# Whole transposes beside each other in two mixtures of experts, and second-half weights fetched from DRAM tile by tile

## The chip, the core and the metric

One Trainium2 chip, of which the kernel uses one core. A core has TensorE (PE, matrix products and transposes), VectorE (DVE), ScalarE (ACT), GpSimd (POOL) and SyncE (SP), each with an instruction stream of its own. They meet only at semaphores. Sixteen DMA engines move data between DRAM and the on-chip memory (SBUF). Accumulators lie in eight PSUM banks. The metric is device microseconds (us) of one launch, lower is better.

## The reference

The input x has 4 x 256 rows of 256 numbers (1,024 tokens). Four steps add to it in turn: an attention-like map, a first mixture of experts, an edge map, a second mixture. All is float32. Only the two mixtures matter here (cut):

```
# first mixture: 8 experts of width 688, the best 2 for each token
g = einsum('th,efh->etf', xf, gate_w); u = einsum('th,efh->etf', xf, up_w)
y = einsum('etf,ehf->eth', silu(g) * u, down_w)
out = einsum('te,eth->th', combine, y)

# second mixture: 15 experts of width 176, the best 2, and one shared expert for all
for i in range(15):
    y = y + (silu(xf @ w1[i].T) * (xf @ w3[i].T) @ w2[i].T) * combine[:, i:i+1]
z = silu(xf @ sw1.T) * (xf @ sw3.T) @ sw2.T
```

Each mixture normalizes its input rows first, and its result is scaled by a gate and added to x.

## The kernel before

**Tiles and halves.** A mixture sorts the (token, expert) pairs by expert and cuts them into tiles of 128 slots. Each tile has two halves of 64 slots, and each half belongs to one expert, so that a tile has a first and a second expert. The first mixture has S0 = 20 tiles, the second S1 = 23. The tables `owner` (experts of the halves), `tok` (which row a slot reads) and `dst` (where its result goes) are made on the chip.

**One tile.** POOL gathers 128 rows from DRAM into `x_in` (`gather`, L402). PE transposes them into PSUM bank 6 (`turn_x`), DVE copies that to `xT` (`copy_xT`, L1007), PE multiplies by gate and up weights (`gate_up0` or `gate_up1`), ACT takes the tanh (`tanh_half`), DVE makes the hidden row (`hidden`), PE transposes it (`turn_h`), ACT (and DVE in the first mixture) copies it to `hT`, PE multiplies by the down weights (`down`), ACT copies the result to `y_sb`, and POOL scatters it to DRAM (`scatter`, L408).

**Halves side by side.** PE computes a tile's two halves with separate weights: each product is a pair, one using 64 columns of the array for the first half (FIRST), one the other 64 for the second (SECOND). Each float32 product of such a kind appears as two records. In the first mixture a transpose is one instruction over 128 columns (`turn`, L1165; `nc.tensor.transpose`, L1323). In the second it is cut like the products: `turn_rows` (L1299) makes two products of 64 columns with the identity.

**Two copies of the address.** All weights of the 8 or 15 experts lie in SBUF (`wgu`, `wdn`). The first half reads them in place, at an offset held in a PE register. The second half reads a staged copy at a fixed place. In the second mixture DVE copies 704 numbers per partition for gate and up (`stage_gate_up1`, L1024) and ACT 512 for down (`stage_down1`, L684), two buffers each. In the first mixture `stage_gate_up0` and `stage_down0` do this with one buffer; the change leaves them.

**Order of the work.** It is written out by hand for each engine. PE in the first mixture, step s (L1384): `turn_h(s)`, `gate_up0(s+1)`, `turn_x(s+2)`, `down0(s)`. In the second, step s (L1457): `turn_h(s)`, `gate_up_slots(s+2)`, `turn_x(s+3)`, `down(s)`. A second mixture step reads registers with `value_load` (L1344) ahead of gate-up and of down. After its 23 tiles come four tiles of the shared expert; four others were done before. `turn_x(t)` waits for its gathered rows and for the copy of tile t-1's transpose, as all share bank 6. `gate_up(t)` waits for `xT_copied`, `t+1` times. POOL's order in a step is gather (six or seven tiles ahead), then scatter.

**SyncE.** SP loads the experts' weights of the first mixture, stores rows, loads the second mixture's weights while the first runs (L356), and after the second mixture waits for all scatters (L371) and loads the results (L375). During the second mixture's steps it has nothing to do. `rows<-sums` (L369) loads 256 KB per transfer, `wgu<-results` (L376) loads 512 KB per transfer.

Of the kernel before, what the change touches and what calls it, by code (L numbers as in the profile page):

```python
# [14 lines left out]
P = 128  # L15
# [3 lines left out]
NS = NT // 2  # L19
# [20 lines left out]
FC0, FC1 = 120, P  # L40
# [48 lines left out]
def build(nc, x, xt, small, vecs, router, const_f, const_h, gu0, wd0, gu1, wd1, out):  # L89
# [16 lines left out]
    with ctx:  # L106
# [63 lines left out]
        stage_gu1 = wgu[:, spare:spare + 2 * GU1].rearrange("p (r f) -> p r f", f=GU1)  # L170
        stage_dn1 = wgu[:, spare + 2 * GU1:spare + 2 * GU1 + 2 * WD1].rearrange("p (r f) -> p r f", f=WD1)
# [63 lines left out]
        class Mixture:  # L235


            def __init__(m, n, experts, tiles, chunks, wide, ahead):
# [23 lines left out]
                m.y_stored = [sem(f"y_stored{n}{r}") for r in range(RING)]  # L262
# [3 lines left out]
                m.gu_staged, m.dn_staged = sem(f"gu_staged{n}"), sem(f"dn_staged{n}")  # L266
# [53 lines left out]
        def _(sp):  # L320
# [156 lines left out]
        def _(act):  # L477
# [206 lines left out]
            def stage_down1(t):  # L684

                expert = second_owner(m1, t)
                nc.scalar.activation(stage_dn1[:, t % 2, :], wdn[:, bass.ds(expert * WD1 + WD1, WD1)],
                                     ACT.Copy).then_inc(m1.dn_staged, 1)

            act.wait_ge(m1.experts_ready, 1)  # L690
            for n, (_, gu_a, gu_z, dn_a, dn_z) in enumerate(second_weights()):
                act.wait_ge(w1_here[n], 16 * (gu_z > gu_a) + 16 * (dn_z > dn_a))
            stage_down1(0)
            stage_down1(1)
# [3 lines left out]
            def step1(s, r):  # L698
# [17 lines left out]
        def _(dve):  # L716
# [307 lines left out]
            def stage_gate_up1(t):  # L1024

                expert = second_owner(mix[1], t)
                nc.vector.tensor_copy(stage_gu1[:, t % 2, :], wgu[:, bass.ds(expert * GU1 + GU1, GU1)]
                                      ).then_inc(mix[1].gu_staged, 1)

# [18 lines left out]
            def step0(s, r):  # L1048
                copy_hT(m, s, r)
                if s < m.S - 2:  # L1050
                    expert = second_owner(m, s + 2)
                    weights_of(dve, expert, s + 2)
# [6 lines left out]
                if s < m.S - 2:  # L1059
                    copy_xT(m, s + 2, r % 2)  # L1060
# [60 lines left out]
            dve.wait_ge(m1.experts_ready, 1)  # L1121
            for n, (_, gu_a, gu_z, dn_a, dn_z) in enumerate(second_weights()):
                dve.wait_ge(w1_here[n], 16 * (gu_z > gu_a) + 16 * (dn_z > dn_a))
            stage_gate_up1(0)
            stage_gate_up1(1)
# [4 lines left out]
            stage_gate_up1(2)  # L1130
            copy_xT(m1, 2, 0)
            hidden(m1, NS + 1, 1, m1.half)
            stage_gate_up1(3)

            def step1(s, r):
# [4 lines left out]
                if s < m1.S - 4:  # L1140
                    stage_gate_up1(s + 4)
# [20 lines left out]
        def _(pe):  # L1162
# [136 lines left out]
            def turn_rows(dst, src):  # L1299

                for part in (FIRST, SECOND):
                    last = mm(dst[part, :], src[:, part], ident, start=True, stop=True)  # L1302
                return last

            def turn_x(m, t, r):
# [3 lines left out]
                for k in range(KH):  # L1309
                    if m.n == 0:  # L1310
                        last = turn(psum[6][:, k * P:(k + 1) * P], x_in[:, r, k * P:(k + 1) * P])
                    else:
                        last = turn_rows(psum[6][:, k * P:(k + 1) * P], x_in[:, r, k * P:(k + 1) * P])
                last.then_inc(m.xT_done, 1)

            def turn_h(m, s, r):
# [3 lines left out]
                for j in range(m.chunks):  # L1320
                    bank, col = (4, j * P) if j < 4 else (5, (j - 4) * P)
                    if m.n == 0:
                        last = nc.tensor.transpose(psum[bank][0:m.wide, col:col + P],  # L1323
                                                   rows[:, j * m.wide:(j + 1) * m.wide], cf[:, C_ID:C_ID + P])
                    else:
                        last = turn_rows(psum[bank][:, col:col + P], rows[:, j * P:(j + 1) * P])
# [85 lines left out]
            def gate_up_slots(t, r):  # L1412
                at = owner(m1, t) * GU1 + GU1
                pe.wait_ge(m1.xT_copied, t + 1)
                pe.wait_ge(m1.gu_staged, t + 1)
                gate_up1(r, xT[:, r, :], lambda k: wgu[:, bass.ds(at + k * 2 * F1, 2 * F1)],
                         lambda k: stage_gu1[:, t % 2, k * 2 * F1:(k + 1) * 2 * F1])
# [18 lines left out]
            def down_shared(t):  # L1436

                def weights(j):
                    return wdn[:, j * H:(j + 1) * H]
# [17 lines left out]
            def step1(s, r):  # L1457
                turn_h(m1, s + NS, r % 2)
                if s < m1.S - 2:
# [3 lines left out]
                if s < m1.S - 3:  # L1463
                    turn_x(m1, s + 3, (r + 3) % RING)
# [3 lines left out]
                if s < m1.S:  # L1468
                    at = owner(m1, s) * WD1 + WD1
                    pe.wait_ge(m1.dn_staged, s + 1)  # L1470
                    down(m1, s + NS, lambda j: wdn[:, bass.ds(at + j * H, H)],
                         lambda j: stage_dn1[:, s % 2, j * H:(j + 1) * H])
# [80 lines left out]
```

## Time and profile before

| what | value |
|---|---|
| median of 3 runs | 384.3 us (381.86 to 384.68) |
| the profiled execution's own time | 386.76 us, span 385.0 us |
| PE busy | 332.4 us (86%), 2,484 instructions |
| DVE, ACT, POOL busy | 207.5, 152.3, 121.8 us |
| chain that ended last | PE 75%, DVE 10%, DMA 6%, issue 4%, ACT 2%, POOL 2% |
| moved by DMA | 49.47 MB, mean 129 GB/s |
| mean granted TensorE clock | 0.89 of full speed |

Times in rows count from the span's start. The first mixture's steps run from about 65 to 235 us, the second's from about 296 to 377. A PE record is as long as one instruction from its first column to its modelled end, and neighbours overlap: what an instruction costs is the distance to the next start. "x8" joins eight records. "PEld" is a weight load, which may run ahead of the products. In brackets stands how long the engine sat idle before it and what ended that. "issue" is idle time for which the profile shows no releaser.

### The profile page before, as it was taken

The numbers are of one execution on the slowest core, as the hardware profiler recorded it, in microseconds if no ns is written. First come the engines' busy times: TensorE is split into PE (matmuls) and PEld (weight loads), VectorE is DVE, ScalarE is ACT, GpSimd is POOL, SyncE is SP. The second block draws the span as 40 slices with busy tenths as digits, with TensorE's granted clock in tenths as the row PEclk, the third lists the DMA queues.
The fourth block names the chain that finished last, engine by engine and source line by source line (L and its number), as shares of the span: only waits on it lengthen the run. The fifth ranks groups of instructions, "written<-read, shape, count | busy, mean of one in ns | idle before, by whom it ended". The sixth has DMA issues, their size and how long they took to land.

```text
span 385.0 us, 7592 instructions
## 1 busy us (share of the span) xinstructions
PE 332.4 (86%) x2484; PEld 200.6 (52%) x2484; DVE 207.5 (54%) x639; ACT 152.3 (40%) x322; POOL 121.8 (32%) x118
## 2 busy tenths in 40 slices
PE   8966589999999999999999996049839999999991
PEld 6635454555555555555555554037525666666560
DVE  2678874445555544445555531783863444445337
ACT  1555221333333334433333344363611444445441
POOL 0022050214232223322211113230662677765320
PEclk9995558999999999999999999555975999999996
DMA  7999739993211271122216885321011222222136
GB/s 245 338 328 287 254 106 319 280 267 77 39 30 29 41 223 30 27 40 32 28 15 219 273 296 126 110 69 41 0 49 49 70 84 84 81 80 63 55 129 227
DMA packets 21659, 49.47 MB, mean 129 GB/s; under 512 B 2600, under 2 KB 11688, under 8 KB 20600
## 3 DMA queue, kind: packets, MB, share of 16 engines
q1 hardware_dynamic: 15192, 36.83, 29.5%
q0 software_dynamic: 6048, 11.28, 13.7%
q10 hardware_dynamic: 384, 0.90, 0.7%
q8 instruction: 22, 0.36, 0.4%
q14 instruction: 13, 0.11, 0.1%
HBM read 39.03 MB, written 9.96 MB: 127 GB/s over the span
## 4 chain that ended last, share of the span: by engine, by line
PE 75%; DVE 10%; DMA 6%; issue 4%; ACT 2%; POOL 2%; DVEq 0%; POOLq 0%; ACTq 0%; SPq 0%
PE bank L1361 24%; PE bank L1335 19%; PE bank L1401 10%; PE bank L1302 6%; PE bank L1323 4%; PE bank L1167 3%; DMA sums<-y_sb,route_dst 3%; PE bank L1227 2%; PE bank L1175 2%; DVE st L737 2%; DMA wgu<-results 1%; DVE z L815 1%; DVE rows L1068 1%; DMA x_in<-rows,route_tok 1%; PE bank L1247 1%
## 5 line engine op out<-in xcount | busy, mean ns | idle before, releaser
L1361 PE MATMUL bank<-wgu,xT 128*64 x320 | 99.8, 466 | 1.4 <-DVE xT L1010 1.3
L1361 PE MATMUL bank<-rows,xT 128*64 128x344 f32 x320 | 99.8, 466 | 0.0
L1335 PE MATMUL bank<-wdn,hT 120*64 (+2 forms) x396 | 88.3, 383 | 5.2 <-ACT hT L589 4.9
L404 POOL DMA_INDIRECT x_in<-rows,route_tok x43 | 43.0, 1000 | 90.1 <-PE bank L1167 58.1
L1361 PEld LDWEIGHTS bank<-wgu,xT 128*64 128x64 f32 x320 | 43.2, 140 | 47.7 <-issue 8.6
L1335 PEld LDWEIGHTS bank<-wdn,hT 120*64 120x64 f32 (+1 forms) x396 | 47.6, 137 | 31.0 <-issue 9.9
L1335 PE MATMUL bank<-rows,hT 120*64 120x256 f32 x240 | 56.0, 383 | 0.0
L412 POOL DMA_INDIRECT sums<-y_sb,route_dst x20 | 31.6, 1580 | 76.5 <-ACT y_sb L625 58.5
L990 DVE SCALAR_TENSOR_TENSOR hh<-th,bank 128x344 f32<-128x344 f32 x40 | 20.5, 513 | 60.9 <-ACT th L578 60.9
L1361 PEld LDWEIGHTS bank<-rows,xT 128*64 128x64 f32 x320 | 43.2, 140 | 0.0
L578 ACT ACTIVATE th<-bank 128x344 f32<-128x344 f32 x40 | 18.3, 457 | 56.1 <-PE bank L1361 56.1
L1401 PE MATMUL bank<-wgu,xT 128*64 (+1 forms) x184 | 34.8, 502 | 3.5 <-issue 1.6
L1021 DVE COPY rows<-wgu 128x688 f32 x78 | 36.7, 513 | 1.2 <-issue 1.2
L1010 DVE COPY xT<-bank 128x256 f32<-128x256 f32 x43 | 18.1, 421 | 29.1 <-PE bank L1302 29.0
L416 POOL DMA_INDIRECT results<-y_sb,route_dst x23 | 28.1, 1220 | 17.3 <-ACT y_sb L706 12.4
L1335 PEld LDWEIGHTS bank<-rows,hT 120*64 120x64 f32 x240 | 31.3, 137 | 0.0
L601 ACT ACTIVATE rows<-wdn 120x1536 f32 x20 | 29.7, 1483 | 4.0 <-issue 4.0
L625 ACT ACTIVATE y_sb<-bank,route_share 128x256 f32<-128x256 f32 x20 | 9.5, 474 | 53.1 <-PE bank L1335 50.9
L1167 PE MATMUL bank<-cf,rows 128*128 128x128 f32 x40 | 10.2, 386 | 20.3 <-ACT rows L514 14.6
L589 ACT ACTIVATE hT<-bank 128x256 f32<-128x256 f32 (+1 forms) x51 | 23.1, 452 | 3.7 <-PE bank L1323 2.1
L1335 PE MATMUL bank<-wgu,hT 128*64 128x256 f32 x92 | 23.8, 381 | 0.0
L994 DVE TENSOR_TENSOR hh<-hh,bank 128x344 f32<-128x344 f32 x40 | 20.5, 512 | 1.4
(156 smaller groups left out, 475.5 us busy)
## 6 DMA issues: line engine op xcount, KB each, us to landing
wgu<-gu SPq DMA_DIRECT2D x8, 1376.0 KB, 23.1
wdn<-wd SPq DMA_DIRECT2D x8, 720.0 KB, 27.2
wgu<-gu SPq DMA_DIRECT2D x3, 1408.0 KB, 6.4
wdn<-wd SPq DMA_DIRECT2D x5, 768.0 KB, 9.7
rows<-rows SPq DMA_DIRECT2D x8, 256.0 KB, 3.7
wgu<-results SPq DMA_DIRECT2D x4, 512.0 KB, 5.3
wgu<-gu SPq DMA_DIRECT2D x1, 1056.0 KB
rows<-xt SPq DMA_DIRECT2D x4, 256.0 KB, 7.2
```

The lines of the kernel that those rows point to most:

```text
L404: nc.gpsimd.indirect_dma_start(out=x_in[:, t % RING, :], out_offset=None, in_=rows, in_offset=bass.IndirectOffsetOnAxis(ap=m.tok[:, t:t + ...
L412: nc.gpsimd.indirect_dma_start(out=sums, out_offset=bass.IndirectOffsetOnAxis(ap=m.dst[:, s:s + 1], axis=0), in_=y_sb[:, s % RING, :], in_ ...
L416: nc.gpsimd.indirect_dma_start(out=results, out_offset=bass.IndirectOffsetOnAxis(ap=m.dst[:, s:s + 1], axis=0), in_=y_sb[:, s % RING, :], ...
L589: nc.scalar.activation(hT[0:m.wide, 0:n], psum[4][0:m.wide, 0:n], ACT.Copy, scale=0.5 / UNITS if m.n == 0 else 0.5).then_inc(m.hT_copied_a, 1)
L601: nc.scalar.activation(stage_dn0[0:FC0, :], wdn[0:FC0, bass.ds(expert * WD0, WD0)], ACT.Copy).then_inc(mix[0].dn_staged, 1)
L990: nc.vector.scalar_tensor_tensor(out=hh[:, cols], in0=th[:, cols], scalar=1.0, in1=psum[2 * c][:, 0:CH0], op0=ALU.add, op1=ALU.mult).then_ ...
L1021: nc.vector.tensor_copy(kept_gu[:, k, :], wgu[:, bass.ds(expert * GU0 + (k * 4 + 2 * c) * CH0, 2 * CH0)]).then_inc(mix[0].gu_staged, 1)
L1167: return nc.tensor.transpose(dst, src, cf[:, C_ID:C_ID + P])
L1302: last = mm(dst[part, :], src[:, part], ident, start=True, stop=True)
L1335: last = mm(psum[7][part, 0:H], hT[0:m.wide, j * P:(j + 1) * P][:, part], wd(j), start=(j == 0), stop=(j == m.chunks - 1))
L1361: last = mm(psum[2 * c + g][part, 0:CH0], xT[:, r, k * P:(k + 1) * P][:, part], w, start=(k == 0), stop=(k == KH - 1))
L1401: last = mm(psum[r][part, 0:2 * F1], src[:, k * P:(k + 1) * P][:, part], w(k), start=(k == 0), stop=(k == KH - 1))
```

## The change

Four edits.

1. In the first mixture PE's `turn_x(s+2)` moves from behind `gate_up0(s+1)` to directly behind `turn_h(s)`. DVE's `copy_xT(s+2)` moves ahead of the hidden rows of its step.
2. In the second mixture `turn_rows` goes; `turn_x` and `turn_h` use whole transposes, and `turn_x(s+3)` moves directly behind `turn_h(s)`. The hidden width is cut in two chunks of 96 instead of 128, so that `wd1` has 96 partitions, and its loads shrink from 768 to 576 KB.
3. DVE's and ACT's staging copies of the second mixture go. SP loads the second expert's weights from DRAM instead: 352 KB for gate and up, 192 KB for down, per tile, into three buffers.
4. PE waits for these loads instead of for the copies. Each load has a semaphore for its buffer.

```
+                    sp.wait_ge(m.experts_ready, 1)
+                    for t in range(m.S):
+                        expert = sp.value_load(m.owner[0:1, bass.ds(2 * t + 1, 1)], min_val=0, max_val=m.E - 1)
+                        if t >= 3:
+                            sp.wait_ge(m.gu_done, NS + t - 2)
+                        sp.dma_start(stage_gu1[:, t % 3, :], gu1[bass.ds(expert + 1, 1)].rearrange("e p n -> p (e n)")
+                                     ).then_inc(m.gu_here[t % 3], 16)
+                        if t >= 3:
+                            sp.wait_ge(m.y_done, NS + t - 2)
+                        sp.dma_start(stage_dn1[0:FC1, t % 3, :], wd1[bass.ds(expert + 1, 1)].rearrange("e p n -> p (e n)")
+                                     ).then_inc(m.dn_here[t % 3], 16)
...
-                    if s < m1.S - 2:
-                        stage_down1(s + 2)
...
             def step0(s, r):
                 copy_hT(m, s, r)
                 if s < m.S - 2:
+                    copy_xT(m, s + 2, r % 2)
...
-                if s < m1.S - 4:
-                    stage_gate_up1(s + 4)
...
                 turn_h(m, s, r)
+                if s < m.S - 2:
+                    turn_x(m, s + 2, (r + 2) % RING)
                 if s < m.S - 1:
                     gate_up0(s + 1, (r + 1) % 2)
-                if s < m.S - 2:
-                    turn_x(m, s + 2, (r + 2) % RING)
                 down0(s, r)
...
-                pe.wait_ge(m1.gu_staged, t + 1)
+                pe.wait_ge(m1.gu_here[t % 3], 16 * (t // 3 + 1))
...
                 turn_h(m1, s + NS, r % 2)
+                if s < m1.S - 3:
+                    turn_x(m1, s + 3, (r + 3) % RING)
                 if s < m1.S - 2:
                     gate_up_slots(s + 2, r % 2)
...
-                    pe.wait_ge(m1.dn_staged, s + 1)
+                    pe.wait_ge(m1.dn_here[s % 3], 16 * (s // 3 + 1))
```

`gu_done` and `y_done` count finished gate-ups and downs. With the NS = 4 shared tiles ahead, both waits of round t mean tile t-3.

## Rows read from the trace of the kernel before

**Rows 1.** Windows: one stretch of the second mixture; engines' busy us, PEclk, DMA share, GB/s

```profile
320.00:365.00 45.00, 43.77 (x446) 28.29 (x444) 20.65 (x55) 22.68 (x58) 26.90 (x24) 1.00 0.24 72
```

**Rows 2.** Timeline of PE, one step of the first mixture: start us, us, instruction

```profile
134.53 0.87 PE L1323 MATMUL bank<-cf,hh 128*120 128x128 f32 x6
...
135.33 0.50 PE L1361 MATMUL bank<-wgu,xT 128*64 x1
...
139.72 0.45 PE L1361 MATMUL bank<-wgu,xT 128*64 x1
...
140.11 0.44 PE L1167 MATMUL bank<-cf,x_in 128*128 128x128 f32 x2
...
140.48 0.43 PE L1335 MATMUL bank<-wdn,hT 120*64 x1
...
140.74 0.38 PE L1335 MATMUL bank<-wdn,hT 120*64 x1
...
142.69 0.38 PE L1335 MATMUL bank<-wdn,hT 120*64 x1
...
142.90 0.38 PE L1335 MATMUL bank<-wdn,hT 120*64 x1
...
143.22 0.87 PE L1323 MATMUL bank<-cf,hh 128*120 128x128 f32 x6
```

**Rows 3.** Timeline of DVE in the same step: the last hidden half

```profile
141.26 0.51 DVE L994 TENSOR_TENSOR hh<-hh,bank 128x344 f32<-128x344 f32 x1
```

**Rows 4.** Timeline, one step of the second mixture: PE, PEld, DVE, ACT

```profile
328.45 1.40 PE L1401 MATMUL bank<-wgu,xT 128*64 x8
...
329.68 0.61 PE L1302 MATMUL bank<-cf,x_in 128*64 128x128 f32 x8
...
330.12 0.38 PE L1335 MATMUL bank<-wdn,hT 128*64 x1
...
330.98 0.61 PE L1302 MATMUL bank<-cf,kv 128*64 128x128 f32 x8
331.09 0.42 DVE L1010 COPY xT<-bank 128x256 f32<-128x256 f32 x1 [1.25 <-PE bank L1302]
331.20 0.38 ACT L706 ACTIVATE y_sb<-bank 128x256 f32<-128x256 f32 x1 [0.60 <-PE bank L1335]
...
331.67 0.79 PEld L1401 LDWEIGHTS bank<-wgu,xT 128*64 128x64 f32 x8 [0.32 <-issue]
```

**Rows 5.** Timeline of PE: the last pair of down in tile 0 and in tile 22

```profile
298.90 0.38 PE L1335 MATMUL bank<-wdn,hT 128*64 x1
...
367.82 0.38 PE L1335 MATMUL bank<-wdn,hT 128*64 x1
```

**Rows 6.** Chain that ended last: waits for the first transfer of two bursts

```profile
240.58 3.08 DMA rows<-sums
...
371.46 3.64 DMA wgu<-results
```

**Rows 7.** Timeline of SP: four transfers issued one behind the other

```profile
371.46 1.90 SPq L376 DMA_DIRECT2D wgu<-results  x4
```

**Rows 8.** Chain: ACT reads an expert's number (from 229.68) and uses it as address

```profile
229.68 0.28 ACT y_sb L625
...
230.33 0.17 ACT rows L601
```

**Rows 9.** Page, DMA queues: packets, MB, share of 16 engines over the span

```profile
q1 hardware_dynamic: 15192, 36.83, 29.5%
q0 software_dynamic: 6048, 11.28, 13.7%
```

**Rows 10.** Timeline, start of the second mixture's tiles: DVE, then PE

```profile
283.50 0.18 DVE L932 CAST route_owner<-lower 1x46 int32<-1x46 f32 x1
...
288.11 2.61 PE L1401 MATMUL bank<-wgu,xT 128*64 x8 [1.63 <-issue]
```

**Rows 11.** Windows: a stretch ahead of a fall of PEclk from 1.00 to 0.50 (at 27.3)

```profile
20.40:27.30 6.90, 5.19 (x22) 2.93 (x21) 5.13 (x21) 3.73 (x16) 1.51 (x3) 1.00 1.02 311
```

More of the change, by code:

```diff
@@ L39 @@
 NF0, NF1 = -(-F0 // P), -(-F1 // P)
-FC0, FC1 = 120, P
+FC0, FC1 = 120, 96
 CH0 = F0 // 2
@@ L169, in build @@
         spare = free + 3 * NT * H
-        stage_gu1 = wgu[:, spare:spare + 2 * GU1].rearrange("p (r f) -> p r f", f=GU1)
-        stage_dn1 = wgu[:, spare + 2 * GU1:spare + 2 * GU1 + 2 * WD1].rearrange("p (r f) -> p r f", f=WD1)
+        stage_gu1 = wgu[:, spare:spare + 3 * GU1].rearrange("p (r f) -> p r f", f=GU1)
+        stage_dn1 = wgu[:, spare + 3 * GU1:spare + 3 * GU1 + 3 * WD1].rearrange("p (r f) -> p r f", f=WD1)
         psum = [ctx.enter_context(nc.psum_tensor(f"bank{i}", [P, 512], fp32)) for i in range(8)]
@@ L261, in __init__ @@
                 m.y_done, m.y_copied = sem(f"y_done{n}"), sem(f"y_copied{n}")
-                m.y_stored = [sem(f"y_stored{n}{r}") for r in range(RING)]
                 m.y_here = [sem(f"y_here{n}{b}") for b in range(B)]
@@ L265, in __init__ @@
                 m.half = sem(f"half{n}")
-                m.gu_staged, m.dn_staged = sem(f"gu_staged{n}"), sem(f"dn_staged{n}")
+                if n == 0:
+                    m.gu_staged, m.dn_staged = sem("gu_staged"), sem("dn_staged")
+                else:
+                    m.gu_here, m.dn_here = [sem(f"gu_here{r}") for r in range(3)], [sem(f"dn_here{r}") for r in range(3)]
+                    m.y_stored = [sem(f"y_stored{r}") for r in range(RING)]
                 W, k2 = experts, 2 * NT
@@ L683, in _ @@
                     route_exps(m1)
[L684 to L694, printed above, removed]
             tanh_half(m1, NS, 0)
@@ L1022, in stage_gate_up0 @@
                                           ).then_inc(mix[0].gu_staged, 1)
[L1024 to L1028, printed above, removed]
             m = mix[0]
@@ L1059, in step0 @@
                 if s < m.S - 2:
-                    copy_xT(m, s + 2, r % 2)
                     stage_gate_up0(s + 2, expert, 1)
@@ L1119, in _ @@
             route(m1)
[L1121 to L1125, printed above, removed]
             copy_xT(m1, 0, 0)
@@ L1129, in _ @@
             hidden(m1, NS, 0, m1.half)
-            stage_gate_up1(2)
             copy_xT(m1, 2, 0)
             hidden(m1, NS + 1, 1, m1.half)
-            stage_gate_up1(3)
             def step1(s, r):
@@ L1297, in _ @@
             FIRST, SECOND = slice(0, HALF), slice(HALF, P)
[L1299 to L1303, printed above, removed]
             def turn_x(m, t, r):
@@ L1309, in turn_x @@
                 for k in range(KH):
[L1310 to L1313, printed above, removed]
+                    last = turn(psum[6][:, k * P:(k + 1) * P], x_in[:, r, k * P:(k + 1) * P])
                 last.then_inc(m.xT_done, 1)
@@ L1321, in turn_h @@
                     bank, col = (4, j * P) if j < 4 else (5, (j - 4) * P)
[L1322 to L1326, printed above, removed]
+                    last = nc.tensor.transpose(psum[bank][0:m.wide, col:col + P],
+                                               rows[:, j * m.wide:(j + 1) * m.wide], cf[:, C_ID:C_ID + P])
                 last.then_inc(m.hT_done, 1)
@@ L1414, in gate_up_slots @@
                 pe.wait_ge(m1.xT_copied, t + 1)
-                pe.wait_ge(m1.gu_staged, t + 1)
+                pe.wait_ge(m1.gu_here[t % 3], 16 * (t // 3 + 1))
                 gate_up1(r, xT[:, r, :], lambda k: wgu[:, bass.ds(at + k * 2 * F1, 2 * F1)],
-                         lambda k: stage_gu1[:, t % 2, k * 2 * F1:(k + 1) * 2 * F1])
+                         lambda k: stage_gu1[:, t % 3, k * 2 * F1:(k + 1) * 2 * F1])
             for i in range(NT):
@@ L1438, in weights @@
                 def weights(j):
-                    return wdn[:, j * H:(j + 1) * H]
+                    return wdn[0:FC1, j * H:(j + 1) * H]
                 down(m1, t, weights, weights)
@@ L1462, in step1 @@
                     gate_up_shared(r % 2, xnT[:, NS + s + 2 - m1.S, :])
-                if s < m1.S - 3:
-                    turn_x(m1, s + 3, (r + 3) % RING)
                 if s == 0:
@@ L1469, in step1 @@
                     at = owner(m1, s) * WD1 + WD1
-                    pe.wait_ge(m1.dn_staged, s + 1)
-                    down(m1, s + NS, lambda j: wdn[:, bass.ds(at + j * H, H)],
-                         lambda j: stage_dn1[:, s % 2, j * H:(j + 1) * H])
+                    pe.wait_ge(m1.dn_here[s % 3], 16 * (s // 3 + 1))
+                    down(m1, s + NS, lambda j: wdn[0:FC1, bass.ds(at + j * H, H)],
+                         lambda j: stage_dn1[0:FC1, s % 3, j * H:(j + 1) * H])
                 else:
```

## The prediction

> **What bounds the kernel now.** I read the chain of waits first, then windows over the second mixture, then the timeline of one step in each mixture. In both mixtures the chain runs along PE. In the second, PE is busy 43.8 of 45 us at the full clock while DVE and ACT stand half idle and the DMA engines are used to 0.24 [rows 1]. So the staging copies that the change removes are beside PE, not on the path: by themselves they are worth nothing. What pays is what PE gains; what can cost is a load that PE must now wait for.
>
> **First mixture: the transposes.** A step lasts 143.22 - 134.53 = 8.69 us [rows 2]. Six transposes take 135.33 - 134.53 = 0.80 until gate-up starts, two take 140.48 - 140.11 = 0.37 until down starts. So one costs (0.80 - 0.37)/4 = 0.1075, and each visit to the transposes leaves 0.80 - 0.645 = 0.155 behind it. Ahead of it there is more: gate-up's 16 pairs follow each other by (139.72 - 135.33)/15 = 0.29, `turn_x` follows the last by 0.39, so 0.10 is lost on entering. The first pair of down behind it takes 0.26 where the others take 0.21. Now `turn_x` lies beside `turn_h`: one visit of eight in place of two. Per step that saves 0.155 + 0.10 + 0.05 = 0.30 us, leaving 8.39. It holds in steps 0 to 17, which have a `turn_x`: 18 x 0.30 = **-5.4 us**.
>
> Covered: hidden rows are needed by the next `turn_h`. DVE ends the last one at 141.77 [rows 3], 1.76 after gate-up's end (139.72 + 0.29 = 140.01). Gate-up is now followed by down alone, 12 pairs x 0.215 = 2.58, so 0.8 remains. DVE's earlier `copy_xT` falls into an idle stretch ahead of the hidden rows, and POOL's gathers, six tiles ahead, are only released earlier. Bounds: 0 if DVE or a gather is late after all, -6 if entering and leaving cost somewhat more than I read.
>
> **Second mixture: what PE has to do.** Before, a step is 331.67 - 328.45 = 3.22 [rows 4]: gate-up 1.23, `turn_x` 0.44, down 0.86, `turn_h` 0.44 (four of its pairs, like `turn_x`), and 0.25 of waiting for `copy_xT`, which DVE only starts at 331.09. After: four whole transposes in one visit, 0.10 + 4 x 0.1075 + 0.155 = 0.69, then 1.23 + 0.86: 2.78. Nothing waits for `copy_xT`, as it is made a whole gate-up and down ahead. Without `turn_x` it is 2.57. If the weights were always there, the stretch from the end of tile 0's down to that of tile 22's, 68.9 us before (367.82 - 298.90) [rows 5], would be 20 x 2.78 + 2 x 2.57 = 60.7. POOL, 26.9 busy in some 14 steps, or 1.9 a step [rows 1], allows that, as gathers run seven tiles ahead.
>
> **Second mixture: the load in the loop.** SP issues in the order gate-up(t), down(t), gate-up(t+1). Down(t-1) needs the buffer of tile t-4, so it waits for `y_done` of tile t-4, and gate-up(t), though its own buffer has been free for longer, is queued behind it on SP. PE wants gate-up(t) in step t-2. Between the end of down(t-4) and that point lie one step and the transposes, 2.78 + 0.69 = 3.47. What has to happen in that time:
> - until SP sees the end of down(t-4): ACT sees it at 331.20, 0.22 after down has made way for `turn_h` at 330.98 [rows 4].
> - issue of down(t-1), 1.90/4 = 0.47 [rows 7].
> - reading the expert's number: ACT needs from 229.68 to 230.33 for that, 0.65 [rows 8]. SP has not done it before. I take the same.
> - turning it into two DRAM addresses, and the test on `gu_done`: no row shows this. Bounds 0.1 and 0.9; I take 0.4. Together SP needs 1.5 (1.2 to 2.0).
> - issue to landing of 352 KB: 256 KB took 3.08 and 512 KB 3.64 [rows 6], so 3.29 by their slope; with a gather or the down load beside it a little more. I take 3.3, bounds 3.0 and 4.2.
> - 0.13 until PE's first pair runs, an estimate.
>
> That is 0.22 + 1.5 + 3.3 + 0.13 = 5.15 against 3.47: the load is late by 1.7 us. The loop closes over two steps: those 5.15, then gate-up 1.23 and down 0.86, make 7.24 us for two steps, 3.62 for one, against 3.22 before. Three buffers don't help, since SP's one queue ties the load of gate-up to the end of a down. Tile 4 is the first so bound and tile 22 the last, wanted in step 20: ten rounds from the end of step 0. So 10 x 7.24 + 2 x 2.57 = 77.5 in place of 68.9: **+8.6 us**. The load of down has two steps more and hides. Without staging, DVE and ACT are only freer.
>
> The Trainium skill ("DMA: Bandwidth & Descriptors", section "Anatomy of one DMA", a fit for transfers issued by GpSimd) gives 2.0 us and the bytes at 436 GB/s, an estimate of 2.8 us for 352 KB. By it the stage would cost 4.7 us less than I say, and the sum below would be -2.2. The rows have already 3.08 for the smaller transfer, so I go by them.
>
> **Start and end.** The experts are known at 283.68, and PE's first slot gate-up starts at 288.11, behind DVE's two copies [rows 10]. Now SP reads the number and issues (0.65 + 0.2), and 3.3 later the weights are there: 287.9. Later the shorter transposes at the half clock give a little in two rounds: -0.7 for the end of tile 0 (0 to -1.5). The first three loads have free buffers. The tail (scatter, loads of results, sums) keeps its order: 0. Smaller `wd1` loads in the first mixture are hidden: 0.
>
> **Sum.** -5.4 + 8.6 - 0.7 = +2.5 us. The profiled execution, span 385.0 and own time 386.8, would be 387.5 and 389.3. It lies 2.4 over the median of 384.3, which becomes **386.8**. With SP and landing at their low ends (1.2 + 3.0) a double step is 6.64 and the sum -3.5; at their high ends (2.0 + 4.2) 8.64, sum +16.5.
>
> **Rivals.**
> - *The load comes nearly in time* (chance 0.20). For it: SP is otherwise idle, and the engines' mean use is 0.24 [rows 1]. If landing and SP's work fall to 3.1 together, PE never waits: 60.7 - 68.9 = -8.2, in all -14.3, **370**. That needs a landing well under any row. Halfway, at 6.4 for two steps, the sum is -5.9, 378.
> - *The DMA engines are short* (0.22, slower). 544 KB of weights a step at q1's rate (36.83 MB in 0.295 x 385 us = 324 GB/s) is 1.72 us, and gather and scatter, 256 KB at q0's rate (214 GB/s), 1.22 [rows 9]: 2.94 of a 3.62 us step. If each gate-up load has to let one step's gather and scatter by, it lands 1.2 later, two steps are 8.44, and the stage grows by 20.6: sum +14.5, **399**. Against it: in the second mixture 0.24 of 3.22, or 0.77, carries the gather and scatter, less than 1.22. It decides from the point where landing passes 4 us.
> - *The clock falls* (0.06, slower). In one stretch PE was busy 5.19 of 6.9 us at full clock, and then it fell to half [rows 11]. The new stage has 2.78 of 3.62, a like share. At half a step takes about 5.2: if this holds for half of the steps, ten times 1.6, the sum is +18, 403. The Trainium skill ("TensorE: Matmul & The Clock Gate", "What's actually happening") says that throttled is the default and that activity releases it; by it a PE that waits is in danger of just this, and the row agrees as far as it goes.
> - *The merged transposes don't pay* (0.06, slower): PE waits in front of `turn_x` for rows or a copy in the first mixture. Then -5.4 is lost: 392.
> - *It doesn't do what it says*: the wait on `y_done` is met early, since SP runs ahead. The code excludes that from tile 4 on.
>
> **Chances and range.** The forecast has 0.42, its own range 381 to 392; 0.04 are left to what I have not thought of. A change of 1% is 3.8 us, about what a measurement can tell. Under 380.5: the first rival and a little of the forecast, 0.22. Over 388.1: three rivals, 0.34, and the forecast's upper part, 0.07, so 0.41. Between: 0.37. The range reaches from 378, which leaves out most of the first rival, to 399, which takes in most of the DMA case.
>
> **What would show it.** First mixture: 8.39 from `turn_h` to `turn_h`, the two `turn_x` records directly behind the six. Second: PE idle some 1.7 us in front of the gate-up of every other tile, released by a DMA into `wgu`; steps in turn near 2.8 and 4.5; SP's gate-up load issued 1.7 after a down ends and landed 3.3 later. If PE doesn't wait there, the first rival is right. If landings are over 4 us and the DMA share is near 0.8, the second is. If PEclk is 0.5 between 300 and 370, the third. A step over 8.5 in the first mixture would refute my -5.4.

## The result, and the profile after

The changed kernel takes 395.45 us (median of 4 runs, 394.76 to 397.29), the kernel before, run beside it, 384.49 us (4 runs, 381.86 to 384.84). The ratio is 1.0315, 95% interval 1.0277 to 1.0354: slower by 3%. I had forecast 386.8 us in a range of 378 to 399, slower by over 1% being the likeliest of the three cases. Direction and mechanism came out; the size was too small: 11.0 us between the medians where I had 2.5. The time lies outside the forecast's own range of 381 to 392 and nearer to the 399 of the rival with short DMA engines; it was for that rival that the stated range reached up to 399, so the range holds the time by its width more than by the sum. Some executions of a kernel run in a slower state, and the times and ratios of the experiments below are those of the others.

Two windows over the second mixture of the changed kernel (columns as in [rows 1]), and from its page the busy times, SP's DMA queue (packets, MB, share of 16 engines) and the chain of waits by engine:

```profile
296.00:320.00 24.00, 17.49 (x126) 9.01 (x122) 6.84 (x19) 6.45 (x19) 12.60 (x13) 1.00 0.76 214
320.00:365.00 45.00, 33.29 (x236) 17.13 (x232) 12.96 (x36) 12.25 (x35) 19.63 (x20) 1.00 0.74 208
```

```profile
PE 318.5 (81%) x2160; PEld 184.1 (47%) x2160; DVE 196.8 (50%) x616; ACT 139.3 (35%) x299; POOL 116.1 (30%) x118
...
q1 hardware_dynamic: 20568, 48.59, 41.3%
...
PE 54%; DMA 23%; DVE 11%; issue 5%; SPq 3%; ACT 2%; POOL 2%; DVEq 0%; POOLq 0%
```

In the second mixture PE falls from 43.8 to 33.3 us busy of 45, the DMA engines rise from 0.24 to 0.74, and the clock stays full. DMA is now 23% of the chain.

**First mixture**, PE's timeline, the beginning of one step. It answers to [rows 2]:

```profile
131.41 0.87 PE L1299 MATMUL bank<-cf,hh 128*120 128x128 f32 x6
...
132.11 0.38 PE L1153 MATMUL bank<-cf,x_in 128*128 128x128 f32 x2
132.43 0.50 PE L1335 MATMUL bank<-wgu,xT 128*64 x1
```

The two `turn_x` records stand directly behind the six of `turn_h`. The next `turn_h` starts at 139.80, a step of 8.39 us. All steps but the first and the last take that long. The first takes 9.13 where it took 8.89 before, so that all the steps together gain 4.9 us.

**Second mixture**, the timeline of one step, from the last pair of a down and SP's load behind it to the gate-up after the next. It answers to [rows 4]:

```profile
316.01 0.38 PE L1309 MATMUL bank<-wgu,hT 96*64 96x256 f32 x1
...
316.57 0.33 SPq L383 DMA_DIRECT2D wgu<-wd  x1
...
317.66 0.33 SPq L379 DMA_DIRECT2D wgu<-gu  x1
...
317.97 1.40 PE L1375 MATMUL bank<-wgu,xT 128*64 x8 [1.00 <-DMA wgu<-gu]
...
320.17 0.42 PE L1299 MATMUL bank<-cf,kv 128*96 128x128 f32 x2
...
320.42 0.33 SPq L383 DMA_DIRECT2D wgu<-wd  x1
...
320.43 0.38 PE L1153 MATMUL bank<-cf,x_in 128*128 128x128 f32 x2
...
321.51 0.33 SPq L379 DMA_DIRECT2D wgu<-gu  x1
...
321.76 1.40 PE L1375 MATMUL bank<-wgu,xT 128*64 x8 [0.95 <-DMA wgu<-gu]
```

And the end of the stage in the chain of waits:

```profile
363.09 3.83 DMA wgu<-gu
366.92 0.25 issue
367.17 1.40 PE bank L1375 x8
368.57 0.86 PE bank L1309 x8
```

This is the loop of the prediction. A down ends (316.23, its last pair's start and the 0.22 that a pair takes); SP, which waited for that, issues the down load; then it reads the next number and issues the gate-up load, 1.43 us after the end of down; 3.85 us later the weights are there (321.51, the last landing of this load that the trace holds); after 0.25 PE runs gate-up and down, 2.10 us. That is 7.63 us for two steps. The landings come from the trace's record of semaphores; it misses some of the sixteen of most loads of this run, so a landing can be a little later than stated.

Three stretches of the two profiled executions, in us (own times 386.8 and 394.9):

| | before | after | difference |
|---|---|---|---|
| start to end of tile 0's down | 299.12 | 293.67 | -5.45 |
| to the end of tile 22's down (22 steps) | 68.9 | 80.7 | +11.8 |
| to the end of the span | 16.9 | 18.6 | +1.7 |
| span | 385.0 | 393.0 | +8.0 |

The "stage" below is the middle row. The time of before changes a little from chip to chip (380.5 to 384.5), so kernels of different groups are compared by their ratios to before. The expectations' absolute times count from 383 to 385; e7 to e10 ran where the kernel before takes 380.5.

### The profile page after: what moved, and what is told of

Its sections match the earlier page's. It is cut to its first block, busy times and chain, and to the rows that moved or that the text cites. A ratio compares the mean times of both kernels' runs of the same rounds, so it can differ in the third digit from the quotient of the medians.

```text
span 393.0 us, 6917 instructions
## 1 busy us (share of the span) xinstructions
PE 318.5 (81%) x2160; PEld 184.1 (47%) x2160; DVE 196.8 (50%) x616; ACT 139.3 (35%) x299; POOL 116.1 (30%) x118
## 4 chain that ended last, share of the span: by engine, by line
PE 54%; DMA 23%; DVE 11%; issue 5%; SPq 3%; ACT 2%; POOL 2%; DVEq 0%; POOLq 0%
PE bank L1335 21%; PE bank L1309 15%; DMA wgu<-gu 10%; DMA sums<-y_sb,route_dst 7%; PE bank L1375 7%; PE bank L1299 3%; PE bank L1153 3%; PE bank L1213 2%; DMA wgu<-results 2%; DMA rows<-x 2%; DVE st L738 2%; SPq L376 1%; SPq L383 1%; DMA results<-y_sb,route_dst 1%; DVE z L816 1%
## 5 line engine op out<-in xcount | busy, mean ns | idle before, releaser
L1335 PE MATMUL bank<-wgu,xT 128*64 x320 | 98.5, 462 | 2.0 <-DVE xT L1011 1.4
L1335 PE MATMUL bank<-rows,xT 128*64 128x344 f32 x320 | 98.5, 462 | 0.0
L1309 PEld LDWEIGHTS bank<-wdn,hT 120*64 120x64 f32 (+1 forms) x396 | 50.1, 138 | 39.8 <-issue 13.3
L1335 PEld LDWEIGHTS bank<-wgu,xT 128*64 128x64 f32 x320 | 42.7, 138 | 47.2 <-issue 7.4
L1309 PE MATMUL bank<-rows,hT 120*64 120x256 f32 x240 | 56.8, 387 | 0.0
L1375 PE MATMUL bank<-wgu,xT 128*64 (+1 forms) x184 | 33.5, 486 | 22.9 <-DMA wgu<-gu 21.8
L1001 DVE SCALAR_TENSOR_TENSOR kv<-th,bank 128x176 f32<-128x176 f32 x27 | 9.1, 337 | 54.5 <-ACT th L597 50.8
L430 POOL DMA_INDIRECT results<-y_sb,route_dst x23 | 22.7, 986 | 41.6 <-ACT y_sb L709 41.6
L597 ACT ACTIVATE th<-bank 128x176 f32<-128x176 f32 x31 | 9.8, 318 | 68.5 <-PE bank L1375 61.6
L1309 PEld LDWEIGHTS bank<-rows,hT 120*64 120x64 f32 x240 | 33.5, 140 | 0.0
L1375 PEld LDWEIGHTS bank<-wgu,xT 128*64 128x64 f32 x184 | 11.8, 139 | 35.7 <-issue 29.5
```

The source lines that it names most:

```text
L430: nc.gpsimd.indirect_dma_start(out=results, out_offset=bass.IndirectOffsetOnAxis(ap=m.dst[:, s:s + 1], axis=0), in_=y_sb[:, s % RING, :], ...
L1309: last = mm(psum[7][part, 0:H], hT[0:m.wide, j * P:(j + 1) * P][:, part], wd(j), start=(j == 0), stop=(j == m.chunks - 1))
L1335: last = mm(psum[2 * c + g][part, 0:CH0], xT[:, r, k * P:(k + 1) * P][:, part], w, start=(k == 0), stop=(k == KH - 1))
L1375: last = mm(psum[r][part, 0:2 * F1], src[:, k * P:(k + 1) * P][:, part], w(k), start=(k == 0), stop=(k == KH - 1))
```

## The experiments

Loop theory: SP's one queue ties the gate-up load of tile t+4 to the end of tile t's down (the expectation of e7 says t+3, a slip by one tile), and the load's own time then makes the step. Rival: the transfers as such (bytes, engines' share) make it.

### One part alone, and the loop untied

**e2_first_only**: only the first mixture is changed.

```diff
                 if s < m.S - 2:
+                    copy_xT(m, s + 2, r % 2)
...
                 turn_h(m, s, r)
+                if s < m.S - 2:
+                    turn_x(m, s + 2, (r + 2) % RING)
                 if s < m.S - 1:
                     gate_up0(s + 1, (r + 1) % 2)
-                if s < m.S - 2:
-                    turn_x(m, s + 2, (r + 2) % RING)
```

> The kernel before with the first mixture's part of the change alone: turn_x directly behind turn_h, copy_xT ahead of the hidden rows. Loop theory: all of the loss is in the second mixture, this part alone gives -5.4 us (18 steps from 8.69 to 8.39), 379.1. Rival (the first mixture's gain only shows because something else changed, or it is given back at the join of the mixtures): 382 to 385.

Measured: 379.27 us, ratio 0.9892 (0.9845 to 0.9938). Every step but the first (9.13) and the last is again 8.39 us, -4.9 us in all. By the ratio the first mixture's part of the change is worth -4.1 us, with -5.4 inside its interval.

**e1_gu_ahead**: SP issues the gate-up load of the next tile ahead of the down load it used to stand behind.

```diff
-    load_gate_up(t); load_down(t)
+    load_gate_up(t)
+    if t >= 1: load_down(t - 1)
```

(these names stand for the two `sp.dma_start` calls with their waits)

> The changed kernel with one edit: SP issues the load of gate-up(t) ahead of the load of down(t-1), so that it no longer stands behind the wait for the end of down(t-4). Loop theory (the order on SP ties each gate-up load to the end of a down; two steps cost 1.44 + 3.9 + 0.15 + 2.1 = 7.6 us): the load is issued a step earlier, PE has 2 x 2.78 + 0.69 = 6.25 us for 5.5, waits vanish, a step is near 2.78, tile 0's down to tile 22's near 61 to 65 us instead of 80.7: 376 to 380 us. Rival (the DMA engines are short: 544 KB of weights and 256 KB of rows a step): no order helps, a step stays at 3.3 or more, 388 to 396 us.

Measured: 382.06 us, ratio 0.9964 (0.9932 to 0.9995). **e4_dn4** keeps SP's order and gives the down weights four buffers, so that the wait in front of the gate-up load is for a down one tile older.

```diff
-    if t >= 3: sp.wait_ge(m.y_done, NS + t - 2)
+    if t >= 4: sp.wait_ge(m.y_done, NS + t - 3)
```

> The changed kernel with a fourth buffer for the down weights alone; gate-up keeps three and SP's order stays. Loop theory: the wait ahead of gate-up's load is now for the end of down(t-5), a step earlier, so the loads land in time: a step near 2.78, 376 to 380 us. Rival (gate-up's buffers or the DMA engines bound it): as the changed kernel, 393 to 397.

Measured: 381.29 us, ratio 0.9939 (0.9905 to 0.9973). **e5_gu4** gives the fourth buffer to the gate-up weights instead.

```diff
-    if t >= 3: sp.wait_ge(m.gu_done, NS + t - 2)
+    if t >= 4: sp.wait_ge(m.gu_done, NS + t - 3)
```

> The changed kernel with four buffers for the gate-up weights and three for the down weights, SyncE's order kept. Loop theory: the gate-up load of tile t+3 stands in SyncE's queue behind the down load that waits for tile t-1's or t's down, and it is that wait which ties the loads to the step, so a fourth gate-up buffer gives nothing: ratio 1.025 to 1.035 as for the changed kernel. Rival (any further buffer lets the loads run ahead): ratio 0.99 to 1.0, as e4's with four down buffers.

Measured: 392.5 us (two runs), ratio 1.022 (1.0156 to 1.0285). That is a little under the 1.025 to 1.035 expected, which the interval reaches, and far from the rival's 0.99 to 1.0. Its trace is not used here.

The three together decide for the loop. The same bytes, 352 + 192 KB a tile, cost 3% with three down buffers and nothing with four, or with the order turned round. More gate-up buffers leave the kernel slower. The DMA engines are even busier in e1 than in the changed kernel (0.84 against 0.75 of 296 to 356). But both untied kernels miss the forecast of 376 to 380 by one to two us: their stage lasts 68.4 and 68.3 us, and with weights always there it should last about 61. Their PE waits for a gate-up load only once each between 300 and 360 (1.0 and 0.6 us); what it waits for otherwise is the hT copy, 4.1 and 4.3 us in five waits each. (The 65.9 that the expectations of e9 and e12 give for e1 is a misreading by one tile; it is 68.4.)

### The two terms of the loop

**e7_fixed_expert**: SP takes a fixed expert and reads no number (cut):

```diff
-    expert = sp.value_load(m.owner[0:1, bass.ds(2 * t + 1, 1)], ...)
+    expert = 7 + t % 3
```

> SyncE's loads of the second mixture read a fixed expert (7, 8, 9 in turn) in place of the one whose number stands in the owner table, so its number is not read (the output is then another one; the order, the buffers and the bytes are those of the changed kernel). Loop theory (tile t+3's gate-up load is issued only after tile t's down, so two steps last down end to issue 1.44 + landing 3.9 + the two PE pieces): the number read of 0.65 to 0.85 us goes out of the loop once in two steps, 11 times, so -7 to -9 us: 386 to 388 us. Rival (what sets the step is the DMA engines' share, 0.74 busy): an earlier issue lands no earlier, under -2 us: 393 to 395 us.

Measured: 388.2 us, ratio 1.0198 (1.0142 to 1.0254), so 4.5 us below the changed kernel by the ratios. From an end of down to the gate-up issue it is now about 0.57 us in place of 1.44, and the stage has 73.2 in place of 80.7: -7.5, as forecast. Only the kernel gained less. In this profile PE's clock stayed at half for longer. These are the windows of e7 and of the changed kernel over the same 8 us, and tile 0's down ends 2.6 us later in e7:

```profile
288.00:296.00 8.00, 7.59 (x28) 3.25 (x28) 2.11 (x7) 1.01 (x3) 2.26 (x3) 0.50 0.39 120
```

```profile
288.00:296.00 8.00, 6.83 (x46) 3.51 (x48) 3.22 (x10) 1.96 (x6) 3.94 (x5) 1.00 0.53 151
```

**e8_quarter_down**: from tile 3 on SP loads a quarter of the down weights (cut):

```diff
-    sp.dma_start(stage_dn1[0:FC1, t % 3, :], wd1[...])
+    part = WD1 if t < 3 else WD1 // 4
+    sp.dma_start(stage_dn1[0:FC1, t % 3, 0:part], wd1[...][:, 0:part])
```

> The changed kernel, but from tile 3 on SyncE loads only the first quarter of the down weights' columns (48 KB in place of 192 KB; the other columns keep those of an earlier tile, so the output is another one). What made the 352 KB land after 3.9 us where I had put 3.3? Theory A, size only: 144 KB less ahead of it in the queue, at the 0.56 us per 256 KB between the two issues of the kernel before, is -0.3 us per two steps, -3 us: 392 us. Theory B, crowding by the down load and by the gathers and scatters beside it: the landing falls to 3.3 or under, -7 us or more: 388 us or less. If neither (landing stays 3.9): 395 us.

Measured: 389.8 us, ratio 1.0289 (1.0209 to 1.0368), not to be told from the changed kernel by its time. The landings tell more: issue to landing of the 352 KB, 17 of them between 294 and 356, has the median 3.51 us (3.01 to 5.19), in the changed kernel 3.85 (3.20 to 4.22). So about 0.34 of it is the 144 KB ahead of it, as theory A had it; 3.5 is left. One load, issued at 354.72, landed only 5.19 us later, and the timeline shows what that does:

```profile
354.72 0.33 SPq L379 DMA_DIRECT2D wgu<-gu  x1
...
360.25 2.28 PE L1376 MATMUL bank<-wgu,xT 128*64 x8 [2.54 <-DMA wgu<-gu]
```

```profile
359.00:363.00 4.00, 2.75 (x12) 1.41 (x14) 0.09 (x1) 0.32 (x1) 0.00 (x0) 0.70 0.45 125
```

After a wait of 2.54 us the clock fell to half in that window, and gate-up took 2.28 us in place of 1.40. This step lasted 6.2 us, about 2.5 more than its neighbours, which is why the stage (80.1) hides what the shorter landings gained. The rival "the clock falls" is thus a real one, though in the changed kernel the waits of 1.0 us, and one of 2.0 in front of the gate-up at 299.17, left the clock at full.

### Where the untied kernels lose the rest

In e1 steps of 2.77 us alternate with steps of about 3.8. The timeline of e1 over one pair, of each piece the first record only where the others repeat it:

```profile
316.79 1.40 PE L1382 MATMUL bank<-wgu,xT 128*64 x8
...
318.02 0.38 PE L1316 MATMUL bank<-wdn,hT 96*64 x1
...
318.99 0.42 PE L1306 MATMUL bank<-cf,kv 128*96 128x128 f32 x2
...
319.25 0.38 PE L1160 MATMUL bank<-cf,x_in 128*128 128x128 f32 x2
...
319.56 1.40 PE L1382 MATMUL bank<-wgu,xT 128*64 x8
...
320.31 0.32 ACT L604 ACTIVATE th<-bank 128x176 f32<-128x176 f32 x1 [3.25 <-remote]
320.52 0.38 ACT L716 ACTIVATE y_sb<-bank 128x256 f32<-128x256 f32 x1
...
320.78 0.38 ACT L610 ACTIVATE hT<-bank 96x256 f32<-96x256 f32 x1
...
321.80 0.42 PE L1316 MATMUL bank<-wdn,hT 96*64 x1 [0.83 <-ACT hT L610]
```

Gate-up ends at 318.19 by its record, but the tanh that waits for it starts at 320.31. The trace also holds the moments at which semaphores rise: gate-up's at 320.28, down's at 320.38, `turn_h`'s at 320.42, `turn_x`'s at 320.46. Four pieces that ended between 318.2 and 319.6 are reported within 0.18 us, up to 2.1 us late by the records' ends. ACT and DVE stand still meanwhile, and down then waits 0.83 us for the hT copy. Nothing of this is a transfer.

**e9_turn_back**: e1 with `turn_x` of the second mixture back between gate-up and down.

```diff
                 turn_h(m1, s + NS, r % 2)
-                if s < m1.S - 3:
-                    turn_x(m1, s + 3, (r + 3) % RING)
...
+                if s < m1.S - 3:
+                    turn_x(m1, s + 3, (r + 3) % RING)
```

> e1 (gate-up load issued ahead of the down load) with the second mixture's turn_x put back between gate-up and down. In e1's trace every second step lasts 3.8 us in place of 2.77 because the semaphores of gate-up, down, turn_h and turn_x, which follow each other there without a gap, are all reported together about 2.1 us after the gate-up's end. Theory (reports are held while such a gap-free chain of side-by-side pieces runs): the whole transposes between them break the chain, every step is alike at 2.77 + 0.26 for one more visit, 3.0 to 3.1 us, so 22 steps take 66 to 68 us (65.9 in e1) and the kernel 381 to 384 us, and no report is more than 0.9 us late. Rival (the long step comes from the loads): the alternation stays, with one step in two above 3.6 us.

Measured: 378.5 us, ratio 0.9957 (0.993 to 0.9983), stage 67.9. All steps of the stage up to the last ones, which have no `turn_x`, are 3.07 us but for one, and the tanh starts 0.05 us after the gate-up's end:

```profile
316.94 1.40 PE L1382 MATMUL bank<-wgu,xT 128*64 x8
317.05 0.38 ACT L610 ACTIVATE hT<-bank 96x256 f32<-96x256 f32 x1
...
318.27 0.44 PE L1160 MATMUL bank<-cf,x_in 128*128 128x128 f32 x2
318.39 0.32 ACT L604 ACTIVATE th<-bank 128x176 f32<-128x176 f32 x1 [0.96 <-PE bank L1382]
```

The one long step (4.9 us) is a load's, as the waits of PE between 336 and 345 say:

```profile
PE bank L1382 <- DMA wgu<-gu: 1.8, 1, 1.8
```

Otherwise the loads are those of e1 (DMA share 0.83), so they don't make the alternation; the rival is out. The late reports are gone, and one more visit to the transposes costs 0.30 a step: no gain on balance.

**e12_ahead_pause** and **e13_copies_pause** were to put a gap between gate-up's last matmul and down's first weight load, in e1 and in e3 (below).

```diff
+                    pe.wait_ge(mix[0].y_copied, S0)
                     pe.wait_ge(m1.dn_here[s % 3], 16 * (s // 3 + 1))
```

> e1 with one wait more ahead of each of the second mixture's downs on PE, on a semaphore that has long had its value (an instruction of PE's sequencer, about 0.1 us). In e1's long steps down's first weight load stands 0.001 us behind the gate-up's last matmul and the gate-up's semaphore comes 2.1 us late; in the short steps, in the changed kernel and in e10 it stands 0.04 to 0.08 us behind and the semaphore is on time. Theory (the direct succession is what holds the report): the sequencer now arrives 0.1 us later, every report is on time, every step lasts 2.77 to 2.87 us, tile 0's to tile 22's down 60.5 to 62.5 us in place of 65.9, kernel 3.5 to 5.5 us below e1: ratio 0.982 to 0.987. Rival (the loads of 544 KB per step, DMA share 0.86, hold it): a long step in two stays, 65 to 66 us, ratio 0.995.

> e3 (copies by VectorE and ScalarE kept) with the same additional wait as e12. In e3 two steps in three last 2.93 us, the third 3.55, and there the semaphores come 0.3 to 0.9 us late. Theory: 2.93 is ScalarE's loop and stays, the long ones go: tile 0's to tile 22's down 64 to 65 us in place of 68.4, kernel 3.5 to 4.5 us below e3, ratio 0.986 to 0.990. Rival (ScalarE's loop makes the long steps as well): still 67 to 68.5 us, ratio 0.996 to 1.0.

Measured: e12 381.95 us, ratio 0.9927 (0.989 to 0.9964), stage 68.8; e13 383.13 us, ratio 0.9975 (0.994 to 1.0009), stage 69.5. Neither theory's gain came. In e12 the edit did not do what I wanted: the additional wait went into an instruction that was there already, and down's weight load stands as close behind gate-up as before. So e12 tests nothing, and e13 little more: down's load stands 0.39 us behind gate-up in its long steps, as it does in e3 without the wait. But e3 and e13 have late reports (0.9 us) across this gap of 0.39 us, and e10 (below) has reports on time with the load directly behind. (The expectation of e12 gives 0.04 to 0.08 us for e10; its trace has them under 0.01 in all but a few steps.) Direct succession is neither needed nor enough.

### The copies kept, and a better kernel

**e3_copies_kept**: whole transposes side by side in both mixtures, the second mixture's copies by DVE and ACT as before (two buffers each, 96 partitions of down weights).

```diff
-                        last = turn_rows(psum[6][:, k * P:(k + 1) * P], x_in[:, r, k * P:(k + 1) * P])
+                    last = turn(psum[6][:, k * P:(k + 1) * P], x_in[:, r, k * P:(k + 1) * P])
```

(and `turn_h` likewise; `stage_gate_up1` and `stage_down1` stay)

> The changed kernel without its loads: whole transposes and moved turn_x in both mixtures and chunks of 96, but DVE and ACT still stage the second half's weights as before, two buffers each. Loop theory: PE never waits, a second-mixture step is 2.78 us, -5.4 in the first mixture and about -8 in the second: 370 to 372 us. Rival (DVE, ACT or POOL, which needs 0.97 + 1.33 us and two gaps of 0.3 a step, become the bound once a step is under 3): 374 to 377.

Measured: 382.09 us, ratio 0.9976 (0.9945 to 1.0006), stage 68.4. Both expectations missed by more than 5 us. The timeline of e3 over one short step, ACT and the first record of each down:

```profile
325.65 0.42 PE L1329 MATMUL bank<-wdn,hT 96*64 x1 [0.67 <-ACT wgu L687]
...
326.77 0.39 ACT L706 ACTIVATE y_sb<-bank 128x256 f32<-128x256 f32 x1 [1.27 <-issue]
...
327.41 0.63 ACT L687 ACTIVATE wgu<-wdn 96x512 f32 x1 [0.26 <-issue]
...
327.95 0.36 ACT L589 ACTIVATE hT<-bank 96x256 f32<-96x256 f32 x1
...
328.57 0.42 PE L1329 MATMUL bank<-wdn,hT 96*64 x1
```

Down, y copy, number read and copy of the down weights, hT copy, next down: 2.92 us, and PE, which needs 2.77, waits inside that loop. Before the change a step was 3.22 us, with `turn_x` between gate-up and down, and left room for this loop. Every second or third step of e3 is longer still (3.5 to 3.7), with late reports.

**e10_stage_behind**: e3 with ACT's copy of the down weights behind the next hT copy instead of ahead of it.

```diff
                 copy_hT(m1, s + NS, r)
+                if 1 <= s < m1.S - 1:
+                    stage_down1(s + 1)
                 if s < LATE - 2:
                     tanh_half(m1, s + (NS + 2), r % 2)
...
-                    if s < m1.S - 2:
-                        stage_down1(s + 2)
```

> e3 (the whole change, but with the second mixture's copies by VectorE and ScalarE kept) with ScalarE's copy of the down weights moved from behind the y copy to behind the next hT copy. ScalarE theory (in e3 the loop down, y copy 0.39, number read and copy 0.26 + 0.63, hT copy 0.36, down takes 2.93 us and more when something comes late): with the 0.9 us out of that loop PE's own 2.77 us is the bound: 22 steps in 61 to 63 us in place of 68.4, kernel 375 to 377 us. Rival (PE's semaphores are reported late where its pieces follow each other without a gap, as in e1): steps alternate between 2.77 and 3.6 or more, kernel 381 to 383 us.

Measured: 373.18 us, ratio 0.9819 (0.9777 to 0.9861). The best of all: 1.8% under the kernel before, 5% under the changed one. Nineteen steps of 2.77 us, to the hundredth but for the first, stage 60.4. Its window over the second mixture, and its timeline where it can be laid beside e1's:

```profile
296.00:356.00 60.00, 60.00 (x434) 31.13 (x432) 30.29 (x80) 35.38 (x87) 40.13 (x37) 1.00 0.27 82
```

```profile
318.83 0.38 ACT L708 ACTIVATE y_sb<-bank 128x256 f32<-128x256 f32 x1 [0.55 <-PE bank L1329]
...
319.18 0.38 ACT L589 ACTIVATE hT<-bank 96x256 f32<-96x256 f32 x1
319.29 0.20 PEld L1395 LDWEIGHTS bank<-wgu,xT 128*64 128x64 f32 x4 [0.17 <-issue]
319.29 1.41 PE L1395 MATMUL bank<-wgu,xT 128*64 x8
...
319.82 0.63 ACT L687 ACTIVATE wgu<-wdn 96x512 f32 x1 [0.26 <-issue]
...
320.74 0.32 ACT L583 ACTIVATE th<-bank 128x176 f32<-128x176 f32 x1 [0.29 <-PE bank L1395]
```

ACT has the hT copy (319.18) right behind the y copy, the weights' copy after it, and PE is busy 60.00 of 60 us. No copy was removed for this, only one moved by one place in ACT's queue.

**e11_whole_only**: e3 with `turn_x` of the second mixture back in its old place (the edit of e9).

> e3 with the second mixture's turn_x put back between gate-up and down: of the second mixture's change only the whole transposes are left. PE's step is then e9's, 3.07 us, longer than ScalarE's loop of 2.93 and without direct succession of gate-up and down: even steps of 3.07, tile 0's to tile 22's down 66 us (e2, with half-width transposes: 67.9), kernel level with e2 or up to 2 us below it: ratio 0.983 to 0.990. Rival (whole transposes cost more in this place, by their entering and leaving twice a step): steps above 3.15, ratio above 0.991.

Measured: 380.09 us, ratio 0.9889 (0.9848 to 0.9931), stage 69.1, against 67.9 in e2 with half-width transposes. Most steps are 3.07, as forecast; three are 3.6 to 3.9, with late reports around them. So in their old place whole transposes gain nothing on balance: a step without late reports is 3.07 against 3.12 to 3.20 in e2, and the three long ones take that back. The gain of the second mixture comes from having all of them in one visit, and only if ACT's queue then keeps up.

## Why the prediction was right, and where it was too small

- **First mixture, -5.4: the step right, the sum half a us too large.** 8.39 a step was forecast and found in every kernel with the edit, e2 included, which has it alone. But I counted 18 such steps. The first one took 9.13 us in place of 8.89 and the last did not change, so 17 steps gain 5.1, and 4.9 is left.
- **PE-bound step 2.78, stage 60.7: right.** e10 has 2.77 and 60.4; nineteen steps have a `turn_x` behind tile 0's down, not twenty, which makes 60.5 of my 60.7. The working from [rows 2, 4] of what whole transposes cost was good; that PE would get there needed more than weights in time, as e1, e3 and e4 show. A sign stood in [rows 4]: `turn_x` ends by its record at 329.68 + 0.61 = 330.29, yet the copy that waits for it starts at 331.09. I took those 0.8 us as DVE's and did not ask what held them. I had the copies at no cost to anybody ("DVE and ACT are only freer"), which was true of the load version, and a version that keeps them can do as well.
- **The loop: right in mechanism,** by e1, e4 and e5. The wait, its releaser and its place came as written, 1.0 us in front of each gate-up rather than 1.7 in front of every other: the uneven pairs (2.77 and 4.84 at first) level out to 3.8 and 3.8, since a late down delays the next load.
- **The term that was mis-sized is the landing.** I put 3.3 us for issue to landing of 352 KB, from two transfers at [rows 6] that had the queue nearly to themselves. It was 3.85, of which e8 gives about 0.34 to the down load ahead of it. From the end of down to the issue it was 1.44 where I had 0.22 + 1.5; from landing to PE 0.25, not the 0.13 that I had put without a row. So the loop came out 0.4 longer by two terms that were too small (landing, landing to PE) and one that was too large (SP's). The double step is 7.56 on average (7.24), and the stage +11.8 rather than +8.6. The rival "the DMA engines are short" had set its point at landings of over 4 us and a share near 0.8. The trace has 3.85 and 0.75, so this case lies between the forecast and that rival.
- **Start and end: -0.7 and 0 forecast.** Tile 0's down ends 5.45 earlier, not 6.1, and it is partly luck that this is so near. The first mixture gives 4.9 of it. Another 1.3 come from ahead of its steps, where no edit stands: they begin at 63.55 in place of 64.83, and anywhere from 61.6 to 64.1 in the other profiles. From the last `turn_h` of the first mixture to the end of tile 0's down it takes 0.7 us more than before, not 0.7 less (and as much more in e2, which has no loads). The first load lands 3.96 us after its issue, not 3.3, and PE's first slot gate-up starts 5.5 us after the experts are known, where it was 4.4 and I had 4.2. The last stretch is 1.7 longer. That stretch is 16.6 to 18.6 us in the profiles of this study, with either kind of transposes, and I have no cause for it.
- **From profile to median.** I took 2.4 off for the profiled execution of before, which lay that far over its median. The changed kernel's lay 0.6 under its own median. These 3.0 us, with 3.2 of the loop, 0.6 of the start and 1.7 of the end, make the 8.6 between 386.8 and 395.45 but for 0.1.
- **The clock: no.** It stayed at 1.00 from 288 to the end of the stage with PE 0.74 busy from 320 to 365. At another place it did fall, behind e8's wait of 2.54 us. The Trainium skill ("TensorE: Matmul & The Clock Gate", "What's actually happening") says that the throttled state is the default and that activity releases it; the trace of e8 agrees.
- **The Trainium skill's fit for one transfer** ("DMA: Bandwidth & Descriptors", "Anatomy of one DMA") is one for transfers issued by GpSimd and gave, as an estimate, 2.8 us for 352 KB, and -2.2 for the sum. The measured median for SP's loads is 3.85, and 3.5 with little ahead of them. The rows decide.

**Still open:** what holds PE's reports back. Shown is that the loads aren't needed for it (e3, e13); that down directly behind gate-up is neither needed (e13) nor enough (e10); and that it went when one copy was moved in ACT's queue (e3 to e10) and when `turn_x` was put back in e1 (e9). The same place of `turn_x` with the copies kept (e11) still has reports 0.4 to 1.0 us late in a few steps, so PE's order alone does not prevent it.

## To carry to other kernels

When a copy is replaced by a load, write down which wait stands ahead of the load in its queue: a third buffer buys nothing if the load is queued behind a wait for the last use of another one. When an operation is moved off PE's path between two others, ask what it covered there; here it had left room for ACT's loop of 2.92 us, and moving one copy of that loop by one place was worth 1.6% of the kernel. Cost a load's landing from a row in which its queue is as full as it will be.

## What the hardware showed that I had not expected

- PE's semaphores can be late by much more than its records say: 0.02 us after the record's end in e10, e9 and almost everywhere in the changed kernel, 0.4 for gate-up and 0.8 for `turn_x` all through the second mixture of the kernel before, 0.9 in e13, 2.1 in e1, and then several at once. The Trainium skill ("Perfetto Trace Analysis", "Tensor Engine Instruction (MATMUL, LD_WEIGHTS)") says that a matmul's end is estimated and that its semaphore is pushed once PSUM has acknowledged the writes; so the record's end is not when others may start. That explains how a gap can be there, but not its size, and no run here shows the acknowledgement itself.
- Entering and leaving whole transposes costs PE about 0.30 us a visit: 3.07 against 2.77 (e9, e10), 8.69 against 8.39 in the first mixture. The Trainium skill ("TensorEngine Tiling (Array Packing)", "Key Properties") says that a change of tiling mode drains the engine; the cost here agrees with that, though no run shows the drain by itself.
- PE can work almost without a gap while DMA brings weights beside it at 0.83 of the engines and 248 GB/s (e9): in the 60 us from 296 on it lost 1.8 us, in one step.
- Reading an expert's number into SP and issuing by it costs about 0.87 us more than a fixed address (1.44 against 0.57 from the end of down to the issue of the gate-up load, the second of the two loads behind it).
